# A recurrent layer's state matrices in two fp16 parts instead of three bf16 parts, with a scale found on the chip

## The reference, cut to what matters

```python
def step(carry, xs):
    h, c = carry
    xi_t, xf_t, xg_t, xo_t = xs
    i_t = jax.nn.sigmoid(xi_t + h @ V_i)
    g_t = jnp.tanh(xg_t + h @ V_c)
    o_t = jax.nn.sigmoid(xo_t + h @ V_o)
    c_new = h * c + i_t * g_t
    h_new = o_t * jnp.tanh(c_new)
    return ((h_new, c_new), h_new)
```

## Time and profile before

| | us |
|---|---|
| median of three runs | 977.14 |
| lowest and highest of them | 975.81, 977.8 |
| the profiled execution, its own time | 982.95 |
| its span | 981.1 |
| recurrence in it, first scan to last | 88.0 to 556.6 |

### The profile page before, as it was taken

One profiled execution on the slowest core, in us unless ns is written; L12 is line 12 of the kernel. 1 busy time (PEld: TensorE's weight loads), 2 busy tenths in 40 slices (PEclk: granted clock), 3 DMA queues, 4 the chain that ended last, 5 costly groups with the idle time before them and its releaser, 6 DMA issues.

```text
span 981.1 us, 23652 instructions
## 1 busy us (share of the span) xinstructions
PE 766.7 (78%) x7705; PEld 515.8 (53%) x7705; DVE 610.1 (62%) x2933; ACT 437.2 (45%) x1595; POOL 305.2 (31%) x468
## 2 busy tenths in 40 slices
PE   0986898888788788888788678777248989999993
PEld 0864554444444444445444356666226666666662
DVE  6235777777777777777777635757625445555552
ACT  1123544444444444444444325445225556666652
POOL 5501122222122122112111114565733333343333
PEclk9995555555555555555555577676559889999997
DMA  5980111111111111111110062541222222222220
GB/s 143 185 245 6 39 33 39 39 34 37 37 32 38 37 32 37 37 33 37 40 40 27 27 194 92 161 137 66 82 81 59 59 70 80 77 81 76 78 65 6
DMA packets 78702, 66.70 MB, mean 68 GB/s; under 512 B 8541, under 2 KB 75364, under 8 KB 78612
## 3 DMA queue, kind: packets, MB, share of 16 engines
q1 hardware_dynamic: 71011, 52.65, 19.5%
q0 software_dynamic: 5984, 12.74, 3.7%
q10 hardware_dynamic: 1642, 0.49, 0.2%
HBM read 40.28 MB, written 27.32 MB: 69 GB/s over the span
## 4 chain that ended last, share of the span: by engine, by line
PE 40%; DVE 25%; ACT 14%; issue 9%; POOL 5%; DMA 4%; SPq 0%; DVEq 0%; POOLq 0%; ACTq 0%
PE pb L764 14%; DVE pb L1389 8%; ACT tanh_c L1063 5%; DVE h L1391 5%; ACT S L1059 5%; POOL xs_d L639 4%; DMA Xp<-xs_d 3%; PE pb L952 3%; PE pb L957 3%; PE pb L972 2%; ACT GC L1061 2%; PE pb L959 2%; PE pb L958 2%; PE pb L916 2%; PE pb L974 1%
## 5 line engine op out<-in xcount | busy, mean ns | idle before, releaser
L764 PEld LDWEIGHTS pb<-h,vp 128*128 128x128 bf16 x3840 | 142.0, 106 | 201.7 <-DVE h L1391 192.6
L764 PE MATMUL pb<-h,vp 128*128 128x32 f16 x3840 | 172.3, 190 | 64.0 <-DVE h L1391 48.1
L1553 DVE SCALAR_TENSOR_TENSOR glo<-Gl,pw,ghi 128x512 f16<-128x512 f32 x91 | 68.4, 752 | 122.9 <-ACT ghi L1180 122.9
L651 POOL DMA_INDIRECT out<-outb,out_i x91 | 89.5, 983 | 161.7 <-DVE outb L1565 158.4
L1059 ACT ACTIVATE S<-pb 128x64 f32<-128x64 f32 x256 | 58.7, 229 | 160.4 <-PE pb L764 158.1
L742 PE MATMUL pb<-xbuf,us 128*128 128x256 f32 x198 | 118.2, 703 | 0.0
L1389 DVE TENSOR_TENSOR_SCAN pb<-S,GC 128x64 f32<-128x64 f32 x256 | 76.8, 300 | 48.5 <-ACT GC L1061 39.2
L1174 ACT ACTIVATE Gl<-pb,pw 128x512 f32<-128x512 f32 x91 | 62.5, 687 | 96.0 <-PE pb L959 96.0
L1063 ACT ACTIVATE tanh_c<-pb 128x32 f32<-128x32 f32 x256 | 50.6, 198 | 93.7 <-DVE pb L1389 93.7
L1391 DVE SCALAR_TENSOR_TENSOR h<-S,tanh_c 128x32 f16<-128x32 f32 x256 | 49.1, 192 | 67.5 <-ACT tanh_c L1063 67.5
L639 POOL DMA_INDIRECT xs_d<-stg,slot x64 | 67.0, 1046 | 53.0 <-DVE slot L1482 36.3
(11 more groups left out here) (316 smaller groups left out, 1699.9 us busy)
## 6 DMA issues: line engine op xcount, KB each, us to landing
Xp<-xs_d SPq DMA_DIRECT2D x91, 130.0 KB, 2.1
adjn<-in_adj SPq DMA_DIRECT2D x32, 256.0 KB, 2.7
x_d<-x2s SPq DMA_DIRECT2D x33, 128.0 KB, 1.8
y_d<-ys SPq DMA_DIRECT2D x33, 128.0 KB, 1.8
yr<-y_d SPq DMA_DIRECT2D x16, 256.0 KB, 3.0
x2r<-x_d SPq DMA_DIRECT2D x16, 256.0 KB, 4.1
X<-in_x SPq DMA_DIRECT2D x4, 912.0 KB, 16.4
xs_d<-zrow SPq DMA_DIRECT2D x1, 3640.0 KB, 13.1
```

The costliest lines, as they stand in the source:

```text
L651: pool.indirect_dma_start(out_rows, bass.IndirectOffsetOnAxis(out_i[t % 4][:, 0:1], 0), outb[t % 4][:], None, bounds_check=B * T - 1, oob_ ...
L764: return mm(o, vp[p][:, q, :], h[:], start=False, stop=True, skip_group_check=True)
```

## The change

- `V` is scaled on the chip by a power of two and split into two fp16 parts instead of three bf16 parts. The power of two comes from the sum of squares of V: ACT squares V with an accumulated sum (new, at the start of its stream), PE adds the partitions with one matmul against ones, ACT copies the result out, and POOL computes from it `hscale` and `hback`, two columns of one value per partition, by 15 small chained instructions; then it scales and splits V.
- `h1` takes two parts of V instead of three, `h2` one instead of two: nine matmuls a step in place of fifteen. `io_ps` comes with the second matmul on `h2` instead of the fourth, `g_ps` with the third instead of the sixth.
- The common scale of the gates is the constant `GS` = 2^14 instead of 1024. The factor on `h` is no longer a constant: `h1`, `hs`, `h * c` and `h_scaled_add` read `hscale` or `hback` from memory as a per-partition operand.
- `setup_ready` moves behind POOL's new chain, which also waits for `gwT_sb`; DVE now waits for it too, once, ahead of the recurrence.

```diff
-            vp = [sb(f"vp{i}", [P, 3, P], BF16, where=rec) for i in range(3)]
+            vp = [sb(f"vp{i}", [P, 3, P], F16, where=rec) for i in range(2)]
...
             pool.wait_ge(ld_lstm, 16 * 10)
-            link(tp.tensor_copy(vp[0][:], V[:]))
-            link(tp.tensor_tensor(Vr[:], V[:], vp[0][:], ALU.subtract))
-            link(tp.tensor_copy(vp[1][:], Vr[:]))
-            link(tp.tensor_tensor(Vr[:], Vr[:], vp[1][:], ALU.subtract))
-            link(tp.tensor_copy(vp[2][:], Vr[:]))
-            link(tp.tensor_scalar(us[:], U[:], SC, None, ALU.mult))
+            link(tp.tensor_scalar(us[:], U[:], GS, None, ALU.mult))
...
-            tp.tensor_copy(ones3[:, P:2 * P], ones[0:3, :]).then_inc(setup_ready, 1)
+            link(tp.tensor_copy(ones3[:, P:2 * P], ones[0:3, :]))
...
+            link(pw(vn[:, 0:1], vn[:, 0:1], vn[:, 1:2], ALU.pow))
...
+            link(ts(hback[:], vn[:, 0:1], 1 / GS, None, ALU.mult))
+            link(pw(hscale[:], hback[:], vn[:, 2:3], ALU.pow))
...
+            link(ts(V[:], V[:], vn[:, 0:1], None, ALU.mult))
+            link(tp.tensor_copy(vp[0][:], V[:]))
+            link(pw(Vr[:], V[:], vp[0][:], ALU.subtract))
+            tp.tensor_copy(vp[1][:], Vr[:]).then_inc(setup_ready, 1)
...
             tr(PB[6][:, 0:P], gw[:], ident)
+            pe.wait_ge(squares_ready, 1)
+            mm(PB[6][:, P + NV:P + NV + 1], ones, vsq[:], start=True, stop=True, skip_group_check=True)
...
                         for q in (0, 1, 2):
-                            for p in range(3):
+                            for p in range(2):
                                 gate(q, p, h1)
                         pe.wait_ge(h2_ready, t + 1)
-                        for q in (0, 1):
-                            for p in range(2):
-                                m = gate(q, p, h2)
-                        m.then_inc(io_ps, 1)
-                        for p in range(2):
-                            m = gate(2, p, h2)
-                        m.then_inc(g_ps, 1)
+                        gate(0, 0, h2)
+                        gate(1, 0, h2).then_inc(io_ps, 1)
+                        gate(2, 0, h2).then_inc(g_ps, 1)
...
+            act.wait_ge(ld_lstm, 16 * 10)
+            av(squared[:, 0:3 * P], V[:].rearrange("p q d -> p (q d)"), ACT.Square, accum_out=vsq[:]).then_inc(squares_ready, 1)
...
+            av(vn[:, 0:1], PB[6][:, P + NV:P + NV + 1], ACT.Copy)
...
+            dve.wait_ge(setup_ready, 1)
...
-                return v.scalar_tensor_tensor(out=x2s[:, i, :], in0=PB[5][:, i * P:(i + 1) * P], scalar=1 / SC,
+                return v.scalar_tensor_tensor(out=x2s[:, i, :], in0=PB[5][:, i * P:(i + 1) * P], scalar=hback[:],
...
-                        v.scalar_tensor_tensor(out=h1[:], in0=S[:, 1, :, 1], scalar=SC, in1=tanh_c[:], op0=ALU.mult, op1=ALU.mult).then_inc(h1_ready, 1)
-                        v.scalar_tensor_tensor(out=hs[k][:, cols], in0=S[:, 1, :, 1], scalar=SC, in1=tanh_c[:], op0=ALU.mult, op1=ALU.mult).then_inc(h32_ready, 1)
+                        v.scalar_tensor_tensor(out=h1[:], in0=S[:, 1, :, 1], scalar=hscale[:], in1=tanh_c[:], op0=ALU.mult, op1=ALU.mult).then_inc(h1_ready, 1)
+                        v.scalar_tensor_tensor(out=hs[k][:, cols], in0=S[:, 1, :, 1], scalar=hscale[:], in1=tanh_c[:], op0=ALU.mult, op1=ALU.mult).then_inc(h32_ready, 1)
...
-                        v.scalar_tensor_tensor(out=GC[:, :, 1], in0=hs[k][:, cols], scalar=1 / SC, in1=CC[:, :, 1], op0=ALU.mult, op1=ALU.mult).then_inc(hc_ready, 1)
+                        v.scalar_tensor_tensor(out=GC[:, :, 1], in0=hs[k][:, cols], scalar=hback[:], in1=CC[:, :, 1], op0=ALU.mult, op1=ALU.mult).then_inc(hc_ready, 1)
```

More of the change, by code:

```diff
@@ L45 @@
 SC = 1024.0
+GS = 2.0 ** 14
 NB2 = B // 2
@@ L182, in build @@
             tick = sb("tick", [P, 2], where=rec)
+            hscale, hback = sb("hscale", [P, 1], where=rec), sb("hback", [P, 1], where=rec)
             deg, degs, dinv, sdiag = (sb(n, [P, 2], where=rec) for n in ("deg", "degs", "dinv", "sdiag"))
@@ L188, in build @@
             Vr = sb("Vr", [P, 3, P], where=pre)
+            vsq, vn = sb("vsq", [P, 1], where=pre), sb("vn", [P, 4], where=pre)
             wst = sb("wst", [P, E, HID], where=pre)
@@ L467, in _ @@
             pool.wait_ge(ld_lstm, 16 * 10)
-            link(tp.tensor_copy(vp[0][:], V[:]))
-            link(tp.tensor_tensor(Vr[:], V[:], vp[0][:], ALU.subtract))
-            link(tp.tensor_copy(vp[1][:], Vr[:]))
-            link(tp.tensor_tensor(Vr[:], Vr[:], vp[1][:], ALU.subtract))
-            link(tp.tensor_copy(vp[2][:], Vr[:]))
-            link(tp.tensor_scalar(us[:], U[:], SC, None, ALU.mult))
-            link(tp.tensor_scalar(bst[:, 0:3, :], bst[:, 0:3, :], SC, None, ALU.mult))
+            link(tp.tensor_scalar(us[:], U[:], GS, None, ALU.mult))
+            link(tp.tensor_scalar(bst[:, 0:3, :], bst[:, 0:3, :], GS, None, ALU.mult))
             link(tp.tensor_copy(bpa[0][:], bst[:]))
@@ L500, in _ @@
             pw = nc.gpsimd.tensor_tensor
+            ts = tp.tensor_scalar
+            link(tp.memset(vn[:, 1:2], 0.5))
+            link(tp.memset(vn[:, 2:3], -1.0))
+            link(pw(vn[:, 0:1], vn[:, 0:1], vn[:, 1:2], ALU.pow))
+            link(ts(vn[:, 0:1], vn[:, 0:1], 1e-9, None, ALU.add))
+            link(pw(vn[:, 0:1], vn[:, 0:1], vn[:, 2:3], ALU.pow))
+            link(ts(vn[:, 0:1], vn[:, 0:1], 2.0 ** 11, None, ALU.mult))
+            link(ts(vn[:, 3:4], vn[:, 0:1], float(2 ** 23 + 1), None, ALU.mult))
+            link(pw(vn[:, 0:1], vn[:, 0:1], vn[:, 3:4], ALU.subtract))
+            link(pw(vn[:, 0:1], vn[:, 0:1], vn[:, 3:4], ALU.add))
+            link(ts(vn[:, 0:1], vn[:, 0:1], 0.5, None, ALU.max))
+            link(ts(hback[:], vn[:, 0:1], 1 / GS, None, ALU.mult))
+            link(pw(hscale[:], hback[:], vn[:, 2:3], ALU.pow))
+            link(ts(vn[:, 3:4], hscale[:], float(2 ** 23 + 1), None, ALU.mult))
+            link(pw(hscale[:], hscale[:], vn[:, 3:4], ALU.subtract))
+            link(pw(hscale[:], hscale[:], vn[:, 3:4], ALU.add))
+            link(ts(V[:], V[:], vn[:, 0:1], None, ALU.mult))
+            link(tp.tensor_copy(vp[0][:], V[:]))
+            link(pw(Vr[:], V[:], vp[0][:], ALU.subtract))
+            tp.tensor_copy(vp[1][:], Vr[:]).then_inc(setup_ready, 1)
             for G in range(2):
@@ L519, in fold_squares @@
             def fold_squares():
-                pool.wait_ge(squares_ready, 9)
+                pool.wait_ge(squares_ready, 10)
                 link(pw(sqh[:], sq[:, :, 0:2], sq[:, :, 2:4], ALU.add))
@@ L1058, in four_groups @@
                         act.wait_ge(io_ps, t + 1)
-                        av(S[:, :, :, 1], io_v[k][:, :, cols], ACT.Sigmoid, scale=1 / SC)
+                        av(S[:, :, :, 1], io_v[k][:, :, cols], ACT.Sigmoid, scale=1 / GS)
                         act.wait_ge(g_ps, t + 1)
-                        av(GC[:, :, 0], g_bank[k][:, cols], ACT.Tanh, scale=1 / SC).then_inc(gates_ready, 1)
+                        av(GC[:, :, 0], g_bank[k][:, cols], ACT.Tanh, scale=1 / GS).then_inc(gates_ready, 1)
                         act.wait_ge(cell_ready, t + 1)
```

## The result

| | before | after |
|---|---|---|
| median, us (lowest to highest) | 977.47 (975.81 to 978.83, 4 runs) | 999.81 (999.23 to 1003.76, 4 runs) |
| ratio, 95% interval | | 1.0238 (1.0207 to 1.0269) |
| the profiled execution, its span | 982.95, 981.1 | 999.23, 997.4 |
| first scan of the recurrence | 88.0 | 87.6 |
| recurrence, first scan to last | 468.6 | 487.7 |

The change makes the kernel 22.3 us slower. Compared once more, it is 22.8 us slower (1000.64 against 977.79, ratio 1.0228, 1.0187 to 1.0269). The recurrence grew by 19.15 us between the two profiled executions, and by 20.0 in the second profile of the kernel after. The two profiled executions themselves are only 16.3 us apart, since that of before took 5.5 us more than its median: the recurrence starts 0.4 us earlier in after, and from its end to the end of the kernel it is 422.1 us (422.0 in the second profile) against 424.5.

The account below looks back on a forecast made before the run. The recurrence was taken as bound by a DVE-PE-ACT ring through h2, 1.81 us a step. 17.7 (28 groups) plus 0.75 (four groups) plus 0.3 (set-up) gave +18.7 us on 977.14, so 995.8 us, range 990 to 1003.

Parts of the forecast that it names:

- The ring: DVE-PE-ACT loop passing through h2, once a step: h2 115 ns later, two matmuls give back 53, sigmoid 62 ns later.
- The price of the operand: Each of five DVE instructions reading a per-partition operand lasts 60 ns longer and delays the next start by 55 ns.
- The step with s = 1: DVE nearly the bound there: 280 ns of new work minus 83 of slack before the scan, +197 ns.
- Rival 3: At s = 1 the scan waits for the statistics instruction's end, no slack: +280 ns, 998.1 us, chance 0.19.
- The first four groups: PE bounds two steps of eight, together -185 ns; the other six lose 62 each: +187 ns a group.
- Set-up: Before the recurrence: PE's extra matmul with ACT's copy +0.3 us (0 to 0.8); POOL's longer chain costs nothing.
- The sum: Whole kernel: 17.7 for 28 groups, 0.75 for four groups, 0.3 for set-up: +18.7 us, median 995.8, chance 0.61.
- the clock behind the recurrence: After the recurrence only the clock's phase changes, left at 1 us either way.
- A sign that was wrong: Profile after: PE's busy time would fall by about a third of L764's.
- Rival 1: Operand read during waits or the previous DVE instruction costs nothing, so the matmuls win: 963.3 us, chance 0.07.
- Rival 2: Half the operand's price on DVE is hidden, 30 ns each: a step loses 7 ns, 979.9 us, chance 0.05.
- Rival 4: Small DVE instructions pay 83 ns instead of 60: a step loses 113 ns, 1011 us, chance 0.08.

Follow-up runs that it names:

- experiment 3: Kernel after with constants in the five DVE instructions and V's second part kept for h2, twelve matmuls: 976.59 us, ratio 0.9984.
- experiment 1: Kernel before, fifteen matmuls untouched, with constants of the five DVE instructions read as per-partition operands: 1011.35 us, ratio 1.0318.
- experiment 4: Kernel before with only hs reading its factor from memory: 990.93 us in one run.
- experiment 2: Kernel after with constants (512 and 1 / 512) back in all five DVE instructions: 969.66 us, ratio 0.9898.
- experiment 6: Kernel after with hscale multiplied onto the o gate by a new DVE instruction, h1 and hs plain products: 1010.63 us, ratio 1.0333.
- experiment 8: Kernel of experiment 6 with the two waits at h1 exchanged, DVE's loop body left at four groups: 991.12 us in one run.
- experiment 7: Kernel of experiment 6 with the two waits at h1 exchanged and DVE's loop body cut to two groups: 969.78 us, ratio 0.9919.
- experiment 9: Same kernel as experiment 2, measured once more against the kernel before: 968.37 us, ratio 0.9881.

## Why the prediction was right

**The ring.** Right in each part. That `h2` and not `h1` is passed through: experiment 3. That `h2` comes 115 ns later: 0.12 measured, 0.061 of it from `hs` and 0.059 from `h1` (experiments 1 and 4). That two matmuls give 53 ns back: experiment 2. Their sum, +62 a step, is +67 in the trace (1.880 against 1.813), since the two operands together cost 120 and not 115. The 55 for the spacing was low by about these 5 ns: 28 x 7 x 0.005 = 1 us.

**The price of the operand.** The pair L1562 and L1323 gave 59 ns and it is 60 (251 and 246 against 191 and 184); `x2s` itself went from 286 to 342, 56 more. The spacing was put at 55 from the earlier trace rows and is 0.168 against 0.109 in the trace, 59. The 83 of the earlier trace rows, from shapes that differ, was no bound that decided anything.

**The step with s = 1.** +0.197 predicted, +0.187 measured, by the predicted mechanism: the row of the scan shows it 0.20 behind the statistics instruction, as the slack of 0.08 had it. Rival 3, that it waits for the end, is refuted by that row. The sentence of the Trainium skill (VectorE: DVE Perf Modes, the section on the drain) that the prediction had set beside it is not the whole rule: the same section goes on that a next operation that is not held starts earlier, and this row agrees with that. With experiment 1 the same 2.000 comes out without any change on PE, which shows that DVE binds there.

**A step that the sum left out.** At s = 4 DVE's other work is nearly as long, and the step takes 1.91: +0.094 instead of +0.062, 28 x 0.032 = 0.9 us. The step with s = 2, behind the long one, loses 0.05 and not 0.062. I had looked at s = 3 as the example for all others. A table of every s would have shown it.

**The first four groups.** +0.75 for the four predicted, +0.50 and +0.88 measured in the two profiles of the kernel after. The two slow steps take 2.05 and 2.12 instead of 2.10 and 2.28, 0.21 less (0.185 predicted); in the first profile the first group has no slow steps, and so the lower sum. There the granted clock was still 0.88 from 87.6 to 92.1 us and 0.50 only from then on, where the kernel before had 0.50 from its first scan; this goes with the missing slow steps, but no run tests it.

**Set-up.** +0.3 predicted, -0.4 measured on the first scan. That neither confirms nor refutes the term: the first scan lies at 87.6 in one profile of this kernel and at 89.0 in the other. The new matmul is on the chain, as a row of the chain that ended last in the kernel after shows, and takes what its neighbour L671 took the earlier trace rows:

```profile
30.92 0.22 PE pb L690 x2
```

POOL's longer chain cost nothing: its last instruction ends at 44.1 us, and POOL is next needed at 80.3.

**The sum.** Recurrence +18.4 predicted (17.7 + 0.75), +19.15 measured. The median moved by 22.3 and not by 18.7. Of the missing 3.6 us, 0.7 lie in the recurrence; the other 3 are in no pair of profiles. The prediction left 1 us either way for the clock behind the recurrence, and this is the term that was sized too small: from the last scan to the end the profiled executions took 417.9 to 428.2 us, though only what is ahead of it differs. 999.81 lies just inside even the narrower 992 to 1000, which had been opened for the price of the operand and not for this term. That the range held is sound for the recurrence, and luck for the rest.

**A sign that was wrong.** PE's busy time was to fall by about a third of that of L764; it fell by 11% (172.3 to 153.5 us). In the step of the earlier trace rows fifteen matmuls keep PE busy for 0.67 us, in the step shown above nine for 0.65, because three of them wait for `h2`. The other signs came: durations, distances, periods, and the clock of 0.50 but for those first 4.5 us.

**Rivals 1, 2 and 4** (operand free, half free, 83 ns) are out by the 251 and 246 ns of L1411 and L1412. The 93 ns that the Trainium skill states for ScalarE (ScalarE: Activation LUTs, the section that times the ACTIVATE instruction) are not DVE's, whose rows show 60; by them a step would have lost 133 ns and not 67.

## What to carry to other kernels

Where a constant becomes a value found at run time, it becomes a per-partition operand, and on DVE each costs its own instruction 60 ns and delays the next start by as much; on a recurrence of 256 steps two of them on the ring cost 30 us. Apply such a factor to an operand that is ready early, in an instruction of its own that lies in a wait, and then look at two more things: that the late wait rides on the instruction itself, and that the loop's body hasn't grown so far that its passes fetch instructions again. Where the engine waits for its last operand, as PE does for `h2` here, removed matmuls count only behind that operand.

## What the runs showed of the hardware that I had not expected

- A backward jump of DVE's loop costs nothing that the trace shows with the body of the kernel before, and 2.7 us each time once the body is 32 products and 32 waits longer (experiments 6 and 8).
- Of two waits in front of one DVE instruction, which one stands by itself is worth 0.073 us a step; the one written first stays on the instruction (experiments 6, 7 and 8).
- The same stretch of the experts' stage runs at a granted clock of 0.84 to 1.00, though its code is the same, and the time from the last scan to the end differs by up to 10 us; the clock goes with a part of this only, and runs of one kernel differ too (experiment 9). The cause is open.
